# Writing the rounded half of the late exponentials on ScalarE instead of casting it on GpSimd

## The reference: two attention layers on eight images

```python
theta, phi, g = conv1x1(x, theta_w, theta_b), conv1x1(x, phi_w, phi_b), conv1x1(x, g_w, g_b)   # 8 x 128 x 1024
attn = softmax(einsum('bcn,bcm->bnm', theta, phi), axis=-1)                                    # 8 x 1024 x 1024
y = einsum('bnm,bcm->bnc', attn, g).reshape(B, Ch, H, W)
z = (1 - w) * x + w * conv1x1(y, wz_w, wz_b)                                                   # result of layer 0
...
q, k, v = Wq @ z + bq, Wk @ z + bk, Wv @ z + bv                                                # 16, 16, 128 channels
att = softmax(q^T k / sqrt(16), axis=-1)
out = gamma * einsum('bcj,bij->bci', v, att)
fused = Wf @ concat([out, z]) + bf
```

## Time and profile before

| | us |
|---|---|
| median of 3 runs | 525.61 (524.16 to 527.09) |
| the profiled execution | 525.3 |
| its span, from the first to the last instruction | 523.5 |
| TensorE busy in the span | 501.3 (96%) |
| VectorE busy | 403.2 (77%) |
| ScalarE busy | 356.3 (68%) |
| GpSimd busy | 307.7 (59%) |

### The profile page before, as it was taken

The page is one execution under the profiler, slowest core; times in us unless marked ns, Lnnn a source line. Parts: engine busy times, 40 slices in busy tenths (PEclk is TensorE's granted clock), DMA queues, the critical chain, the costliest instruction groups (busy, mean ns, idle before and its releaser), DMA issues.

```text
span 523.5 us, 7901 instructions
## 1 busy us (share of the span) xinstructions
PE 501.3 (96%) x2647; PEld 413.0 (79%) x2647; DVE 403.2 (77%) x553; ACT 356.3 (68%) x619; POOL 307.7 (59%) x342
## 2 busy tenths in 40 slices
PE   7898999979999999999999999999999998899996
PEld 5686877858878888888888888888888886777886
DVE  4968685597779977898779968898779867876973
ACT  4756467568775787758785687758785578656763
POOL 1454255667579556966679565975679503744432
PEclk9998999999999999999999999999999999999999
DMA  5010000011000300003000210003000100000001
GB/s 186 17 40 3 0 16 0 2 34 56 8 22 1 100 15 22 2 1 109 8 22 1 92 26 0 21 3 108 10 20 2 40 29 8 2 29 28 22 20 42
DMA packets 18506, 15.30 MB, mean 29 GB/s; under 512 B 12918, under 2 KB 13474, under 8 KB 18466
## 3 DMA queue, kind: packets, MB, share of 16 engines
q1 hardware_dynamic: 18322, 14.67, 9.4%
q10 hardware_dynamic: 144, 0.13, 0.1%
HBM read 8.98 MB, written 4.24 MB: 25 GB/s over the span
## 4 chain that ended last, share of the span: by engine, by line
PE 82%; DVE 6%; ACT 5%; DMA 5%; issue 2%; SPq 0%; POOL 0%; DVEq 0%; ACTq 0%
PE trans L560 12%; PE accum L599 10%; PE accum L601 10%; PE accum L600 10%; PE scores L517 5%; PE scores L543 5%; PE scores L519 5%; PE scores L518 5%; PE trans L570 4%; PE misc L517 3%; PE misc L519 3%; PE misc L518 3%; PE misc L626 3%; DMA turned<-shift_parts 2%; DMA x_keep<-x_dram 1%
## 5 line engine op out<-in xcount | busy, mean ns | idle before, releaser
L882 DVE TENSOR_REDUCE neg_max<-scores 128x1 f32<-128x1024 f32 x128 | 155.3, 1214 | 4.5 <-PE scores L543 3.4
L746 ACT ACTIVATE pt_hi<-trans 128x512 fp32r<-128x512 f32 x168 | 91.8, 597 | 73.1 <-PE trans L560 67.8
L892 DVE TENSOR_TENSOR pt_lo<-trans,pt_hi 128x512 fp32r<-128x512 f32 x168 | 107.8, 682 | 32.3 <-ACT pt_hi L746 30.9
L730 ACT ACTIVATE fulls<-scores,neg_max 128x1024 f32<-128x1024 f32 x84 | 94.3, 1123 | 9.5 <-DVE neg_max L882 9.5
L560 PE MATMUL trans<-ident,fulls 128*128 128x128 f32 x672 | 89.2, 275 | 7.0 <-ACT fulls L730 1.9
L560 PEld LDWEIGHTS trans<-ident,fulls 128*128 128x128 f32 x672 | 75.8, 141 | 18.6 <-ACT fulls L730 6.9
L599 PE MATMUL accum<-pt_hi,g_hi 128*128 128x512 f32 x176 | 70.6, 401 | 1.1 <-DVE o_sb L960 1.0
L601 PE MATMUL accum<-pt_hi,g_lo 128*128 128x512 f32 x176 | 69.1, 393 | 0.0
L600 PE MATMUL accum<-pt_lo,g_hi 128*128 128x512 f32 x176 | 69.0, 392 | 0.0
L899 DVE TENSOR_TENSOR pt_lo<-fulls,pt_hi 128x1024 fp32r<-128x1024 f32 x40 | 53.8, 1345 | 6.3 <-POOL pt_hi L1078 5.2
L1078 POOL CAST pt_hi<-fulls 128x1024 fp32r<-128x1024 f32 x40 | 45.7, 1142 | 20.0 <-ACT fulls L753 19.9
(11 more groups left out here) (186 smaller groups left out, 1041.1 us busy)
## 6 DMA issues: line engine op xcount, KB each, us to landing
x_keep<-x_dram SPq DMA_DIRECT2D x8, 512.0 KB, 3.3
out_dram<-o_sb SPq DMA_DIRECT2D x15, 256.0 KB, 2.0
x_raw<-x_tiles_dram SPq DMA_DIRECT2D x7, 512.0 KB, 3.6
k_op<-qk_op SPq DMA_DIRECT2D x16, 96.0 KB, 2.3
x_raw<-x_tiles_dram SPq DMA_DIRECT2D x2, 256.0 KB, 3.7
turned<-shift_parts SPq DMA_DIRECT2D x22, 2.0 KB, 8.5
w_all<-weights_t_dram SPq DMA_DIRECT2D x1, 336.0 KB, 3.9
out_dram<-o_sb SPq DMA_DIRECT2D x2, 128.0 KB, 1.8
```

The costliest lines, as they stand in the source:

```text
L730: nc.scalar.activation(result, scores[:, k % 2, :], ACT.Exp, bias=neg_max[:, k % 16:k % 16 + 1], accum_out=row_sum[:, slot(gb), t:t + 1]). ...
L746: nc.scalar.activation(pt_hi[:, side(gb), 4 * bank:4 * bank + 4, t * P:(t + 1) * P], trans[:, cols(bank)].rearrange("p (n q) -> p n q", n= ...
L882: nc.vector.tensor_reduce(neg_max[:, k % 16:k % 16 + 1], scores[:, k % 2, :], AX.X, ALU.max, negate=True).then_inc(max_ready, 1)
L892: nc.vector.tensor_tensor(pt_lo[at], trans[:, cols(bank)].rearrange("p (n q) -> p n q", n=4), f(pt_hi[at]), ALU.subtract).then_inc(pt_lo_r ...
```

## The change

ScalarE's `late_exp` of a block other than 24 first waits for the place in `pt_hi`, then takes the exponential of `trans` into `pt_hi`, which is of the rounded type, and raises `late_hi_ready`; after that it takes the same exponential into the ring as before, and only this second one raises `late_ready`. GpSimd's `late_hi` is left out, except for block 24. VectorE's `late_lo` waits for both semaphores.

```diff
             def late_exp(gb, j):
                 act.wait_ge(late_scores_ready, late(gb, j))
                 full_free(act, ("late", gb, j))
+                if gb != ASIDE:
+                    pair_free(act, gb, j)
+                    hi, _ = pair_tiles(gb, j)
+                    nc.scalar.activation(hi, trans[:, :], ACT.Exp).then_inc(late_hi_ready, 1)
                 nc.scalar.activation(full_of(("late", gb, j)), trans[:, :], ACT.Exp).then_inc(late_ready, 1)
...
             def late_lo(gb, j):
                 dve.wait_ge(late_hi_ready, late(gb, j))
+                dve.wait_ge(late_ready, late(gb, j))
                 pair_free(dve, gb, j)
...
                 for gb, j in late_fills(k - 1):
-                    late_hi(gb, j)
+                    if gb == ASIDE:
+                        late_hi(gb, j)
```

## The result

| | before | after |
|---|---|---|
| median of the runs, us | 524.35 (523.66 to 527.09, 5 runs) | 538.31 (537.73 to 540.84, 5 runs) |
| ratio | | 1.0231 (95% interval 1.0188 to 1.0273) |
| profiled execution, us | 525.3 | 540.84 |
| its span, us | 523.5 | 539.0 |

The change costs 14.0 us by the medians. The interval of the ratio, 1.9% to 2.7% of 524.35 us, is 9.9 to 14.3 us. The forecast was 17.7 us on top of 525.6: the time of 538.3 lies within its range of 533 to 554, but the loss was forecast too large.

What follows compares the result with a forecast made beforehand. TensorE, without a gap in the periodic part, was taken as the bound. 5 x 1.24 + 5 x 2.30 = 17.7 us lifts the profiled 525.3 to 543.0, so a median of 543.3 us, 3.4% slower; range 533 to 554.

Steps and rivals of the forecast that it cites:

- TensorE without a gap, so every wait is lost: In the periodic part TensorE is busy 59.98 of 60.00 us, so each microsecond it waits is lost, none given back.
- Cost of an added exponential, 0.92 us, rounded or not: Each of 40 added ScalarE exponentials costs 0.92 us, 36.8 us in all; rounded output takes the same duration.
- Kind 1, 1.24 us at the scores behind the second pair: Five late blocks like block 10: two added exponentials less 0.22 us slack make TensorE's scores start 1.24 us late.
- Kind 2, 2.30 us at the transposes: Five late blocks like block 12: four added exponentials less 1.21 us ScalarE idle start the unit's transposes 2.30 us late.
- Nothing on `pt_lo`, nothing by the dropped casts: The path to `pt_lo` hardly changes, and removing 40 GpSimd casts (45.7 us) gains nothing, as TensorE isn't waiting for it.
- VectorE 1.60 us where GpSimd works beside it and 1.23 where it doesn't: VectorE's subtraction is slowed by GpSimd alongside; even 40 x 0.37 = 15 us less on VectorE would not change the sum.
- What the profile would show: TensorE busy 501 us with idle of 1.2 and 2.3 us per block, period 63.1, ScalarE near 397, GpSimd near 262.
- proportional or full exposure (4): Lag not caught up between late blocks, or held `trans` and late scores chain: 25 to 37 us lost; chance 0.19.
- full absorption (1): The double place of the scores hides ScalarE's lag, TensorE being ahead: 525.6 us; chance 0.06.
- A gain by GpSimd (2): TensorE had inherited VectorE's 5.2 us of waits for GpSimd's casts, which now go: 520.4 us; chance 0.03.
- One gate alone (3): Only one kind's wait bites: kind 2 alone 11.5 us, kind 1 alone 6.2; 537 or 532; chance 0.15.
- The clock (5): TensorE's clock: one more 13 us slice with a tenth less costs 1.3 us; given no case of its own.

Runs made afterwards that it cites:

- first_two: The change made only for the first two pairs of the five kind 1 blocks, against the kernel before: ratio 1.0113, +6.5 us; 1.11 us per kind 1 block.
- extra_ahead: Kernel before, GpSimd's casts kept, plus one extra 128x1024 exponential of a constant into a spare tile ahead of each of 40 late ones: ratio 1.0286, +14.9 us.
- the three amounts of extra work: Kernel before plus an extra exponential of 512, 1024 or 1792 columns ahead of each late one: +1.3, +14.9 and +33.8 us.
- kind1_only: The change made only in late blocks 6, 10, 14, 18, 22, GpSimd casting in the others, against the kernel before: ratio 1.0120, +6.3 us.
- kind2_only: The change made only in late blocks 4, 8, 12, 16, 20, GpSimd casting in the others, against the kernel before: ratio 1.0161, +8.6 us.
- extra_behind: Kernel before, casts kept, plus the extra 128x1024 exponential behind each late one, so `trans` is freed as early as before: ratio 1.0269, +14.1 us.

## Why the prediction was right, and where its sizes were off

The mechanism came as forecast, one gate in each kind and nothing carried over; the size of the loss came out too large by 3.7 us of 17.7. The range was wide, and by itself says little.

- *TensorE without a gap, so every wait is lost*: right but for the 0.23 us told below. The loss of a block is never made up by a later one: with one kind alone changed, the other's blocks stay at 0.0.
- *Cost of an added exponential, 0.92 us, rounded or not*: right. The starts in the change are 0.90 to 0.92 us apart, and the durations are 1029 and 1033 ns.
- *Kind 1, 1.24 us at the scores behind the second pair*: the gate is right (first_two), measured 1.09. The slack ahead of it was under-read: ScalarE's stretch grew by 7.05 - 5.58 = 1.47 us instead of 1.62. The prediction counted one gap; there was a second, too short for a bracket, before the late exponential at 210.71: from the start of the row before (210.33) to it are 0.38 us, after the change 0.26 (216.93 to 217.19).
- *Kind 2, 2.30 us at the transposes*: the gate is right, measured 1.96 there and 1.73 for the block. ScalarE's stretch grew by 2.12 instead of 2.47, the same term: a wait that is filled gives back its idle time and also some 0.1 us of overlap with the row before. The three gave back 0.33, 0.50 and 0.69 us, together 1.52, instead of the 1.21 counted (0.23, 0.39 and 0.59). The other part is the statement that nothing is given back: 0.23 us is, behind the transposes, where by the rows above TensorE had run into VectorE's `pt_lo`.
- *The sum*: 5 x 1.24 + 5 x 2.30 = 17.7 became 5.4 + 8.2 = 13.6 by the trace and 14.0 by the medians. Two of the ten stretches carry a DMA stall removed (1.3 us) or added (0.5). Without the two stalls it is 14.4, and the under-read slack and the 0.23 us account for the 3.3 us between that and 17.7 within some tenths. So the terms that were mis-sized are the two slacks and the nothing given back, and the missing stall made the sum smaller still.
- *Nothing on `pt_lo`, nothing by the dropped casts*: right but for the 0.23 us. Extra_ahead, with all casts in place, costs the same within 0.13 us a block. The shorter mean of VectorE's subtraction, 1278 ns against 1345, can't be put down to the dropped casts: with all casts in place it is 1301 in extra_ahead and 1435 in extra_behind.
- *VectorE 1.60 us where GpSimd works beside it and 1.23 where it doesn't*: misread. GpSimd did run beside the subtraction of 1.23 us, and it was GpSimd that paid (its rows stand with extra_ahead). VectorE is the one held up where an instruction of GpSimd was under way already: at 217.99 that is a cast begun at 217.90, and not the subtraction at 218.60 in the earlier trace rows, which came after. The rule of the Trainium skill on the shared port (SBUF — State Buffer, "Who interferes with whom") agrees with these rows; but in the periodic part TensorE hardly waits for either engine, and the rule says nothing on whether it does.
- *What the profile would show*: the two gates and the counts came as said. Four items didn't. TensorE's busy time was to stay at 501 us and rose to 510.5, since a matmul row is 0.39 us long when the next starts after 0.23: a short delay shows as less overlap and not as idle. Of the 1.96 us in kind 2 only 0.75 + 0.30 stand in brackets. The same kinds are 62.3 us apart (244.60 to 306.94), not 63.1. ScalarE is at 388 us and not 397, since its rows overlap. GpSimd is at 256 us and not 262: other rows of it are shorter too.
- *The rivals*: proportional or full exposure (4) and full absorption (1) are both cut off by the three amounts of extra work. A gain by GpSimd (2) is out by extra_ahead, but for at most 0.23 us in a kind 2 block. One gate alone (3) is out by kind1_only and kind2_only. The clock (5) stayed: the row by slices after is the same as before, one 8 and else 9.

## What to carry to other kernels

An engine's idle time is cover only where it lies between the added work and the instruction that is waited for; count it from row to row up to the next gate, not as a share of the span. An engine that is 73% busy in a period had 0.7 us to spare in one block and 1.7 in the other, and beyond that each us added per pair cost two and four. Where one engine is full, relief on an engine for which it doesn't wait is worth next to nothing: 52 us less on GpSimd here. And a wait that is filled gives back a little more than its idle time, 0.1 us each here, so that a count by the brackets makes the loss too large.

## What the runs showed that was not expected

With the same work on ScalarE, the order decided whether the single place of `trans` was a gate at all: freed ahead of the unit exponential, 0.91 us more per pair cost 14 us, and whether `trans` came free before or after the added work made no difference (extra_ahead, extra_behind); freed only behind the unit exponential, the same work cost 26. And the time to the first late block varied by 4 us from one profiled execution to another (the first late score matmul at 113.97 to 117.90), though the program ahead of it is the same in all of them; a single profile's span should not be read for a few us.
